# The first three tiles projected with a W_in that is not centred, their means corrected later; the second carry one step later

## The reference

```
h   = layernorm(x)                                   # x: [1, 4096, 512]
h   = rmsnorm(h, g_res) @ W_in + b_in                # W_in: [512, 512]
p   = rmsnorm(ctx, g_init)[..., :512]                # ctx: [1, 3202, 1024]
s_i = a * s_(i-1) + b * p_i                          # a scan over the 3202 rows
x1  = x + h + s[plug]                                # plug: from a cumulative sum of the mask
out = x1 + gelu(layernorm(x1) @ w1 + b1) @ w2 + b2   # w1: [512, 2048]
```

## Time and profile before

| | |
|---|---|
| median of 3 executions | 842.86 us (842.5 to 844.9) |
| the profiled execution | 844.34 us, span 842.6 us |
| PE busy | 831.8 us (99%) |
| DVE busy | 317.9 us (38%) |
| ACT busy | 286.4 us (34%) |
| POOL busy | 253.3 us (30%) |
| granted TensorE clock, mean | 0.998 of full speed |

### The profile page before, as it was taken

The page is one execution under the profiler, slowest core; times in us unless marked ns, Lnnn a source line. Parts: engine busy times, 40 slices in busy tenths (PEclk is TensorE's granted clock), DMA queues, the critical chain, the costliest instruction groups (busy, mean ns, idle before and its releaser), DMA issues.

```text
span 842.6 us, 10744 instructions
## 1 busy us (share of the span) xinstructions
PE 831.8 (99%) x3780; PEld 683.9 (81%) x3780; DVE 317.9 (38%) x511; ACT 286.4 (34%) x522; POOL 253.3 (30%) x236
## 2 busy tenths in 40 slices
PE   7998999999999999999999999999999999999998
PEld 5887888888888888888888887888888888888886
DVE  5999762544242334224241514143113311242112
ACT  4664337432432153223522262232222322222221
POOL 2263557950442017200632052203500250002000
PEclk9999999999999999999999999999999999999999
DMA  9858885260216021421224011402300140010001
GB/s 238 252 153 282 228 275 201 91 132 1 75 51 173 0 75 50 131 41 50 74 71 102 21 54 65 82 0 100 50 1 1 56 94 0 0 51 0 1 1 50
DMA packets 34968, 71.07 MB, mean 84 GB/s; under 512 B 5716, under 2 KB 5716, under 8 KB 33176
## 3 DMA queue, kind: packets, MB, share of 16 engines
q1 hardware_dynamic: 25964, 58.91, 21.4%
q0 software_dynamic: 4608, 8.39, 6.5%
q10 hardware_dynamic: 4368, 3.42, 1.5%
HBM read 47.87 MB, written 22.84 MB: 84 GB/s over the span
## 4 chain that ended last, share of the span: by engine, by line
PE 91%; DVE 5%; issue 1%; ACT 1%; DMA 1%; POOL 1%; SPq 0%; ACTq 0%; DVEq 0%; POOLq 0%
PE acc L841 15%; PE acc L843 15%; PE acc L842 15%; PE h_bank L843 14%; PE h_bank L842 14%; PE h_bank L841 14%; PE t_bank L900 2%; DMA win_raw<-in_L_xattn_W_in_dram 1%; DVE st_a L1019 1%; DVE h_lo L1024 1%; DVE cl L1038 1%; PE t_bank L873 1%; PE t_bank L829 1%; DVE cl_next L1038 0%; DVE xa_odd L1032 0%
## 5 line engine op out<-in xcount | busy, mean ns | idle before, releaser
L1241 DVE TENSOR_TENSOR h_lo<-g_f,h_hi 128x512 fp32r<-128x512 f32 x128 | 101.0, 789 | 449.8 <-ACT g_f L778 449.8
L776 ACT ACTIVATE h_hi<-h_bank,b_c 128x512 fp32r<-128x512 f32 x128 | 87.9, 687 | 441.5 <-PE h_bank L843 436.7
L841 PE MATMUL h_bank<-xt_hi,w_hi 128*128 128x512 f32 x512 | 201.8, 394 | 0.0
L841 PE MATMUL acc<-w_hi,h_hi 128*128 128x512 f32 x512 | 199.8, 390 | 0.0
L842 PE MATMUL h_bank<-xt_lo,w_hi 128*128 128x512 f32 x512 | 199.3, 389 | 0.0
L843 PE MATMUL h_bank<-xt_hi,w_lo 128*128 128x512 f32 x512 | 199.3, 389 | 0.0
L843 PE MATMUL acc<-w_hi,h_lo 128*128 128x512 f32 x512 | 199.2, 389 | 0.0
L842 PE MATMUL acc<-w_lo,h_hi 128*128 128x512 f32 x512 | 199.2, 389 | 0.0
L842 PEld LDWEIGHTS h_bank<-xt_lo,w_hi 128*128 128x128 f32 x512 | 96.1, 188 | 20.9 <-issue 1.2
L841 PEld LDWEIGHTS h_bank<-xt_hi,w_hi 128*128 128x128 f32 x512 | 96.2, 188 | 20.9 <-issue 1.2
L843 PEld LDWEIGHTS h_bank<-xt_hi,w_lo 128*128 128x128 f32 x512 | 96.1, 188 | 19.9
(11 more groups left out here) (164 smaller groups left out, 693.9 us busy)
## 6 DMA issues: line engine op xcount, KB each, us to landing
out_dram<-x_cur SPq DMA_DIRECT2D x32, 256.0 KB, 2.1
x_next<-x_part SPq DMA_DIRECT2D x7, 1024.0 KB, 4.9
w_raw<-in_L_ffn_w_dram SPq DMA_DIRECT2D x6, 1024.0 KB, 9.1
scan_table<-cl SPq DMA_DIRECT2D x6, 896.0 KB
ch<-in_ctx_dram SPq DMA_DIRECT2D x20, 256.0 KB, 2.9
cl<-in_ctx_dram SPq DMA_DIRECT2D x5, 1024.0 KB
xa_odd<-in_x_dram SPq DMA_DIRECT2D x16, 256.0 KB, 6.8
x_part<-xa_odd SPq DMA_DIRECT2D x16, 256.0 KB, 4.0
```

The source lines that it names most:

```text
L776: act.activation(h_hi[:, m % HB, :], h_bank[m % 2][:], ACT.Gelu, bias=b1_c[:, m:m + 1])
L841: nc.tensor.matmul(dst, a_hi, b_hi, start=first, stop=False)
L1241: dve.tensor_tensor(h_lo[:, m % HB, :], g_f32[:], h_hi[:, m % HB, :].bitcast(F32), ALU.subtract).then_inc(h_split, 1)
```

## The change

The first three tiles are multiplied with G itself, not with the centred W_in. ScalarE makes `first_hi` = G, rounded, straight from the loaded W_in, and VectorE `first_lo` = W_in * g_res - `first_hi`. GpSimd adds the four blocks of `win_g` up (`add_w_in`), and TensorE sums the result over its rows with one product with `ones` after most of the three tiles' products. ScalarE stores the negative of that sum (`neg_sums`), which serves two purposes: VectorE centres W_in with it for tiles 3 to 31, and ScalarE multiplies it, for each of the three tiles, with mean times `ra` (`scale_sums`, into `mean_part`, which has one buffer), whereupon GpSimd adds it to x (`fix_tile`, into `x_next`) and VectorE's `tile_add` takes that in place of x. Further: x tiles 0, 1, 2 and W_in blocks 0, 3 are issued by SP in turn, blocks 1, 2 by ScalarE; ten warm-up transposes for fourteen; the second block's carry and its additions stand in step 19 in place of 18.

```diff
             for q in range(HP):
                 band_part(q)
             pool.sem_inc(consts_made, 1)
-            for k in (2, 3):
+            def add_w_in(k):
+
+                pool.wait_ge(win_scaled, k + 1)
+                src = win_g[:, 0, :] if k == 1 else win_sum
+                ins = pool.tensor_tensor(win_sum, src, win_g[:, k, :], ALU.add)
+                if k < K - 1:
+                    step(ins)
+                else:
+                    ins.then_inc(win_added, 1)
+
+            def mean_scales(t0, n):
+
+                pool.wait_ge(ra_ready, t0 + n)
+                u = slice(t0, t0 + n)
+                pool.tensor_tensor(mean_ra[:, u], mv_a[:, u, 0], ra[:, u], ALU.mult).then_inc(mean_ra_ready, n)
+
+            def fix_tile(t):
+
+                pool.wait_ge(mean_part_ready, t + 1)
+                pool.tensor_tensor(x_next[:, t, :], xa(t), mean_part, ALU.add).then_inc(x_fixed, 1)
+
+            def late_low_w_in(k):
                 pool.wait_ge(win_hi_done, k + 1)
                 pool.tensor_tensor(win_lo[:, k, :], win_raw[:, k, :], win_hi[:, k, :].bitcast(F32),
                                    ALU.subtract).then_inc(win_lo_late, 1)
+
+            add_w_in(1)
+            add_w_in(2)
+            add_w_in(3)
             scales(0, 2)
+            mean_scales(0, 2)
+            fix_tile(0)
+            fix_tile(1)
+            late_low_w_in(2)
+            late_low_w_in(3)
             scales(2, 2)
+            mean_scales(2, 1)
+            fix_tile(2)
             for t in range(NT):
                 if t == 5:
...
@@ -637,8 +684,8 @@
             own = Tally(act_self)
             act.dma_start(g_res_c[:], g_res.rearrange("(k p) -> p k", p=P),
                           allow_slow_non_contiguous=True).then_inc(g_res_loaded, 16)
-            for t in range(2):
-                act.dma_start(xa(t), x_v[0, :, t, :]).then_inc(xa_loaded[t], 16)
+            for k in (1, 2):
+                act.dma_start(win_raw[:, k, :], win_v[:, k, :]).then_inc(win_loaded[k], 16)
             act.sem_inc(gelu_done, CREDIT)
 
             def load_w1(q):
...
-                act.activation(g_wide[:, k, :], ones[:], ACT.Copy, scale=g_res_c[:, k:k + 1]).then_inc(g_made, 1)
-            for k in range(K):
+
+            def high_first(k):
                 act.wait_ge(win_loaded[k], 16)
+                act.activation(first_hi[:, k, :], win_raw[:, k, :], ACT.Copy, scale=g_res_c[:, k:k + 1]).then_inc(first_hi_done, 1)
+
+            def scale_w_in(k):
                 act.activation(win_g[:, k, :], win_raw[:, k, :], ACT.Copy, scale=g_res_c[:, k:k + 1]).then_inc(win_scaled, 1)
 
             def high_w_in(k):
                 act.wait_ge(win_centred, k + 1)
                 act.activation(win_hi[:, k, :], win_raw[:, k, :], ACT.Copy).then_inc(win_hi_done, 1)
 
+            def scale_sums(t):
+
+                act.wait_ge(mean_ra_ready, t + 1)
+                if t > 0:
+                    act.wait_ge(x_fixed, t)
+                act.activation(mean_part, neg_sums[:], ACT.Copy, scale=mean_ra[:, t:t + 1]).then_inc(mean_part_ready, 1)
+
+            high_first(0)
             tile_high(0)
+            high_first(1)
+            scale_w_in(0)
+            scale_w_in(1)
+            tile_high(1)
+            high_first(2)
+            scale_w_in(2)
+            high_first(3)
+            scale_w_in(3)
+            tile_high(2)
+            act.wait_ge(win_summed, 1)
+            act.activation(neg_sums[:], acc[3][:], ACT.Copy, scale=-1.0).then_inc(neg_sums_made, 1)
+            act.wait_ge(neg_sums_made, 1)
+            scale_sums(0)
             high_w_in(0)
-            tile_high(1)
-            high_w_in(1)
-            tile_high(2)
-            high_w_in(2)
-            high_w_in(3)
             tile_high(3)
+            scale_sums(1)
+            for k in range(1, K):
+                high_w_in(k)
+            scale_sums(2)
             for v, src in ((g_init_b, g_init[0:D]), (b_in_b, b_in), (b2_b, b2)):
                 act.dma_start(v[:], src.rearrange("(a n) -> a n", a=1).to_broadcast([P, D])).then_inc(small_loaded, 16)
             act.dma_start(b1_c[:], b1.rearrange("(m p) -> p m", p=P),
...
@@ -901,22 +967,21 @@
                 ins.then_inc(t_done, 1)
 
             warm_up()
-            sum_w_in(0)
-            sum_w_in(1)
             transpose_first(0)
-            sum_w_in(2)
-            sum_w_in(3)
+            project_raw(0, 0)
             transpose_first(1)
+            project_raw(0, 1)
+            project_raw(1, 0)
+            project_raw(1, 1)
+            project_raw(0, 2)
+            project_raw(1, 2)
             transpose_first(2)
-            for k in (0, 1):
-                project_first_part(0, k)
-                project_first_part(1, k)
-            project_first_part(2, 0)
-            project_first_part(2, 1)
+            project_raw(0, 3)
+            project_raw(1, 3)
+            sum_w_in()
             transpose_first(3)
-            for k in (2, 3):
-                for t in range(3):
-                    project_first_part(t, k)
+            for k in range(K):
+                project_raw(2, k)
             transpose_first(4)
             for t in range(3, NT):
                 if t + 2 < NT:
@@ -928,7 +993,7 @@
                     carry(0, cl, acc[3][:])
                 if t == 16:
                     count_positions()
-                if t == 18:
+                if t == 19:
                     pe.wait_ge(block_ready, 1)
                     carry(1, cl_next, acc[3][:])
                 if t == 20:
...
@@ -1029,7 +1094,10 @@
                 dve.wait_ge(h_used, t + 1)
                 dve.wait_ge(ra_ready, t + 1)
                 u = t % XR
-                dve.scalar_tensor_tensor(x1(t), p_bank[t % 3][:], ra[:, u:u + 1], xa(t), ALU.mult, ALU.add).then_inc(acc_read, 1)
+                if t < RAW:
+                    dve.wait_ge(x_fixed, t + 1)
+                rows = x1(t) if t < RAW else xa(t)
+                dve.scalar_tensor_tensor(x1(t), p_bank[t % 3][:], ra[:, u:u + 1], rows, ALU.mult, ALU.add).then_inc(acc_read, 1)
 
             def scan_row(b, rows, j):
 
@@ -1111,10 +1179,15 @@
             def centre_w_in(k):
 
                 if k == 0:
-                    dve.wait_ge(win_summed, 1)
+                    dve.wait_ge(neg_sums_made, 1)
                 dve.wait_ge(win_scaled, k + 1)
-                dve.scalar_tensor_tensor(win_raw[:, k, :], acc[3][:], -1.0 / D, win_g[:, k, :], ALU.mult, ALU.add)\
+                dve.scalar_tensor_tensor(win_raw[:, k, :], neg_sums[:], 1.0 / D, win_g[:, k, :], ALU.mult, ALU.add)\
                     .then_inc(win_centred, 1)
+
+            def low_first(k):
+                dve.wait_ge(first_hi_done, k + 1)
+                dve.scalar_tensor_tensor(first_lo[:, k, :], win_raw[:, k, :], g_res_c[:, k:k + 1],
+                                         first_hi[:, k, :].bitcast(F32), ALU.mult, ALU.subtract).then_inc(first_lo_done, 1)
 
             def low_w_in(k):
                 dve.wait_ge(win_hi_done, k + 1)
@@ -1159,20 +1232,24 @@
                 dve.tensor_tensor(xt_lo[:, :, i * P:(i + 1) * P], t_bank[i % 2][:].rearrange("p (k r) -> p k r", k=K),
                                   xt_hi[:, :, i * P:(i + 1) * P].bitcast(F32), ALU.subtract).then_inc(t_lo, 1)
 
+            low_first(0)
             tile_low(0)
+            low_first(1)
+            tile_low(1)
+            low_first(2)
+            tile_stats(0)
+            low_first(3)
+            tile_stats(1)
+            tile_low(2)
+            tile_stats(2)
+            tile_stats(3)
             centre_w_in(0)
             centre_w_in(1)
             low_w_in(0)
-            tile_low(1)
             centre_w_in(2)
             low_w_in(1)
             centre_w_in(3)
-            tile_low(2)
-            tile_stats(0)
-            tile_stats(1)
             tile_low(3)
-            tile_stats(2)
-            tile_stats(3)
             for t in range(NT):
                 if t > 0:
                     tile_add(t - 1)
```

More of the change, by code:

```diff
@@ L59 @@
 LAG = 2
-WARM = 14
+WARM = 10
+RAW = 3
 LEAD = 4
@@ L169, in xattn_ffn @@
         win_g = place("win_g", [P, K, D], F32, offset=w_hi_at + 1 * WC * 4)
+        first_hi = place("first_hi", [P, K, D], F32R, offset=w_hi_at + 2 * WC * 4)
+        first_lo = place("first_lo", [P, K, D], F32R, offset=w_hi_at + 3 * WC * 4)
         early_at = [n_rows_at]
@@ L185, in xattn_ffn @@
         ch_next = place("ch_next", [P, R, D], F32, offset=w_hi_at)
+        win_sum = ch[:, 0, :]
+        mean_part = ch[:, 1, :]
         def xa(t):
@@ L202, in xattn_ffn @@
         ident = sb("ident", [P, P])
-        g_wide = early("g_wide", [P, K, P])
+        neg_sums = early("neg_sums", [P, D])
         tri = early("tri", [P, P])
@@ L215, in xattn_ffn @@
         ra = sb("ra", [P, XR])
+        mean_ra = sb("mean_ra", [P, RAW])
         sum_x = sb("sum_x", [P, 2])
@@ L391, in _ @@
             sp.sem_inc(table_stored, STORED)
-            for t in range(2, 8):
```

(10 more changed lines are left out.)

35 lines of the change are left out of this document (21 added, 14 removed).

## The result

The changed kernel takes 849.6 us (median of 9 runs, 847.4 to 851.0), the kernel before 844.9 (9 runs, 842.5 to 846.3, the three known beforehand among them). The ratio is 1.0051, with an interval of 1.0039 to 1.0064. It is slower, as forecast, but by 4.7 us instead of 3.3, and 849.6 lies 0.4 above the range. The profiled execution took 848.73, with a span of 847.0: 4.4 more than the span before.

A forecast was written before the change was run, and what follows sets the result against it. TensorE, busy 831.8 of 842.6 us, was taken as the bound, with only its waits and clock left to win. Late start +5.4, carry -2.1: +3.3 on the median 842.86 gives 846.2 us; range 843.2 to 849.2.

The forecast's parts named there:

- The ring behind the sum: Centring and fixes over ScalarE, VectorE and GpSimd after the sum: project(4) starts at 32.8 instead of 27.92, 4.9 us late.
- S: Moment when the sum of W_in's rows stands in `acc3`: taken as 16.8 us, with 15.9 or 18.4 as alternatives.
- Project(3) at 1.2 GHz is hidden: After 5.9 us idle project(3) takes 5.1 instead of 2.75 us, to 31.8, hidden because project(4) waits for 32.8.
- It cannot catch up by more than 0.1 us: VectorE, 5.9 us late at tile 5's low part, stays late, so TensorE takes over 5.4 us at tile 13.
- The carry, -2.1: Second carry one step later: TensorE's 2.11 us wait up to 76.72 goes, so the full 2.1 us is won.
- The gather, ten steps on, can bear: SP's store of the second block slides 1.5 us behind, which the gather ten steps later was said to bear.
- The base: Time of the kernel before to which the sum was added: the median 842.86 us, giving 846.2.
- The clock rival: TensorE stays at 1.2 GHz through the early products or falls again before project(4): +1.5 to +3 more, 848.7; chance 0.15.

The follow-up runs named there:

- e4: Changed kernel with the centring reading the sum from its PSUM bank instead of the negative copy in SBUF: 847.87 us, ratio 1.0039 to the kernel before.
- e3: Changed kernel with ScalarE's third scaling of the sums moved behind tile 4's high part: 848.51 us, ratio 1.0045 to the kernel before.
- e6: Changed kernel with the third scaling behind tile 4's high part and 48 unread identity transposes ahead of project(3): 847.58 us, ratio 1.0031 to the kernel before.
- e7: Changed kernel with scales(24) split, so the first group's four gathers stand ahead of its second half: 847.85 us, ratio 1.0036 to the kernel before.
- e9: Changed kernel with SyncE's 1 MB load of the third block's low columns in step 26 instead of 25: 849.03 us, ratio 1.0038 to the kernel before.
- e12: Kernel before with only SyncE's 1 MB load of the third block's low columns a step later: 845.92 us, ratio 1.0010.
- e2: The start alone: changed kernel with the second carry back in step 18: 851.59 us, ratio 1.0080 to the kernel before.
- e1: The carry alone: kernel before with the second carry and its four additions in step 19: 842.95 us, ratio 0.9984.
- e8: Kernel before with the second carry a step later and scales(24) split, the gathers ahead of its second half: 842.21 us, ratio 0.9964.
- e10: Kernel before with the second carry a step later and SyncE's 1 MB load in step 26 instead of 25: 841.01 us, ratio 0.9957.
- e11: Changed kernel with third scaling later, centring from PSUM, 48 identity transposes before project(3) and the 1 MB load a step later: 844.91 us, ratio 1.0003 to the kernel before.

## Why the prediction was right in part and wrong in its number

- **The ring behind the sum: right.** Project(3) 26.86 (forecast 26.7), tile 4's high part 31.57 (31.5), project(4) 32.93 (32.8), VectorE's low part of tile 5 34.35 (34.3). e4 and e3 with e6 show that its two causes, blocking and the third scaling in ScalarE's queue, are the true ones.
- **S: right by luck.** It is 16.86, the forecast 16.8. But x0 landed 1.5 us later than taken (first product 8.30 instead of 7.4), and the early products ran at 2.4 GHz, where 16.8 had them at 1.2: two errors that cancel. (The terms from x1 on add up to 5.45 us, not 5.6; it took 5.7.) In the other seven profiles of this order of transfers the early products are slow and S is 17.6 to 19.6, as here in the start alone; the row at 8.30 has 0.50 in the changed kernel's profile:

```profile
8.06 0.79 PE L907 MATMUL acc<-first_hi,h_hi 128*128 128x512 f32 x1 [1.89 <-DVE h_lo L1089]
```

- **Project(3) at 1.2 GHz is hidden: right** (0.92 us of wait left at 32.93; e6).
- **"It cannot catch up by more than 0.1 us": wrong, for 0.4.** VectorE was 5.9 late at tile 5 but only 5.0 at tile 13 (55.61 in rows 12, 60.64 here). So TensorE took nothing over there and stayed at +5.0, not +5.4:

```profile
60.64 0.68 DVE L1089 TENSOR_TENSOR h_lo<-t_bank,h_hi 128x512 fp32r<-128x512 f32 x1
```

- **The carry, -2.1: a size off.** It won 2.4: from the transposes ahead of it to the carry it is 0.43 us now (82.22 to 82.65) and was 2.71 (74.01 to 76.72), 2.28 more, and the carry itself is 0.1 shorter. The 2.11 count from the end of the transposes' row.
- **"The gather, ten steps on, can bear" it: the step that failed.** I counted the slack in steps of the program, and for the store alone. The gathers hang on VectorE's statistics through scales(24) on GpSimd, and on what else is in the queues. I read no row of theirs, and the sum has them at nothing. What the runs showed in its place: the gathers land up to 11.5 us after their issue, beside SyncE's load, and TensorE waits for them, 1.6 us here (e7 and e9: the wait goes) and 2.6 in the carry alone.
- **The base: 2 us too low.** I set the sum on the median of three runs, 842.86, though the profiled execution took 844.34; over nine runs the median is 844.9. On the profiled time the forecast would have been 847.6. Together: 842.86 + 2.0 (base) + 3.3 - 0.4 - 0.3 + 1.6 = 849.1, of 849.6. The base alone is a larger part of the miss than the gathers. The last 0.5 is open; the profiled execution is 0.9 below the median, and its S is the earliest of eight.
- **The clock rival** (848.7) has nearly the time. In the changed kernel's profile its mechanism is absent: S was not delayed and project(4) not slowed. Its first half, slow early products, is there in the other seven profiles; how often in the nine timed executions, no trace shows.

## What to carry to other kernels

When a wait is removed from the bottleneck engine, everything downstream must be earlier by as much; look at the next transfers it depends on, what their issue hangs on and what is in flight beside them, and move the big load that nobody needs yet (e12: a step later it may itself be what is waited for). Where two causes end at the same moment (here an engine's queue and a low clock), each looks free and neither pays alone: remove both. A head start at the beginning of a pipeline is worth only what the serial chain behind it lets through.

## What the hardware showed that I had not expected

Waits of nearly the same length had different prices in clock. In the kernel before, 2.11 us of idle before the carry left the clock at 1.00 and the products 0.23 us apart. In the start alone 2.18 us (at 82.67) and in e12 2.27 us (at 78.28) brought it down to 1.2 GHz; the stretches behind the waits, of the kernel before, of e2 and of e12:

```profile
78.00:80.00 2.00, 2.00 (x11) 1.60 (x10) 1.79 (x7) 0.00 (x0) 0.00 (x0) 1.00 1.01 364
```

```profile
84.00:86.00 2.00, 2.00 (x6) 1.56 (x5) 1.79 (x7) 0.00 (x0) 0.00 (x0) 0.50 1.03 386
```

```profile
80.00:82.00 2.00, 2.00 (x6) 1.61 (x5) 1.86 (x6) 0.00 (x0) 0.00 (x0) 0.50 1.09 367
```

Eight products 0.43 apart cost 1.6 us more. The wait of 1.98 us at 12.99 did so before; in e1, e8 and e10 that wait was 1.39 us, in e12 1.55, and the clock stayed up. The spread of the times fits in part: beside e10 the kernel before has 842.9 to 846.4 us, e10, without the long wait at the carry, 840.5 to 841.5; but e11, without it too, has 843.2 to 846.6. By the Trainium skill (TensorE: Matmul & The Clock Gate, "Part 1: The HAM clock gate") the chip judges activity on a clock of its own that doesn't start with the kernel, so that the outcome varies between runs. The varying outcome is in these traces; that this is its reason, no run here shows. The waits for the normalized rows differ as well: behind 2.12 us in e3 the clock was 0.51 (124.0 to 127.0), behind 2.63 us in the carry alone 1.00 (116.7 to 119.0). Of these six waits of 2.0 to 2.6 us four were worth their length and some 1.6 us more, and two their length alone.

The second block's store (896 and 96 KB) is slow too. In e8 SyncE issued it from 85.82, and GpSimd, waiting for it, started its gathers only at 94.61:

```profile
94.61 1.80 POOL L540 DMA_INDIRECT x_next<-scan_table,idx  x1 [4.03 <-DMA scan_table<-cl_next]
```
